# A routed feed-forward block with attention on one core: the first tile's copy, the late slots and two residual sums in another order

## The reference

```
x = x + 0.5 * ffn(layernorm(x))
x = x + attention(layernorm(x))        # 16 heads of 16, 4 key/value groups, causal
x = x + 0.5 * ffn(layernorm(x))

ffn(h):  route = sigmoid(h @ router_w)               # 8 experts
         e     = argmax(route), p = max(route)
         out   = p * (silu(h @ gate_w[e]) * (h @ up_w[e])) @ down_w[e]
```

## Time and profile before

| | us |
|---|---|
| median of three runs | 398.64 |
| lowest and highest run | 398.38, 400.58 |
| span of the profiled execution, first to last instruction | 397.6 |
| PE busy | 361.3 (91%) |
| DVE busy | 242.6 (61%) |
| POOL busy | 169.8 (43%) |
| ACT busy | 142.5 (36%) |

### The profile page before, as it was taken

How to read it: one execution, slowest core, us unless ns; L and a number is a source line. 1 busy time by engine, 2 the same in 40 slices (tenths; PEclk the granted TensorE clock), 3 DMA queues, 4 the chain that set the end, 5 groups by cost and what they waited for, 6 DMA issues and landing times.

```text
span 397.6 us, 8485 instructions
## 1 busy us (share of the span) xinstructions
PE 361.3 (91%) x3149; PEld 293.3 (74%) x3149; DVE 242.6 (61%) x773; ACT 142.5 (36%) x300; POOL 169.8 (43%) x291
## 2 busy tenths in 40 slices
PE   8679999999999778898999999899899999999980
PEld 4439999999967346576676666676599999999670
DVE  4887864222332766887989779789847874332220
ACT  2312111111120334675676757576434111111110
POOL 2040333565213243467767655565802424663111
PEclk9879999999999998999999999998989999999995
DMA  8959871249701644423616154100210111399100
GB/s 260 411 192 329 298 252 54 67 150 343 275 25 48 199 116 83 87 54 64 106 25 128 53 77 83 50 27 29 85 37 27 41 41 46 95 357 350 37 17 21
DMA packets 28099, 50.07 MB, mean 126 GB/s; under 512 B 4812, under 2 KB 21584, under 8 KB 27026
## 3 DMA queue, kind: packets, MB, share of 16 engines
q1 hardware_dynamic: 20082, 24.89, 22.7%
q0 software_dynamic: 4592, 21.76, 15.8%
q10 hardware_dynamic: 3376, 2.80, 2.4%
HBM read 34.95 MB, written 6.82 MB: 105 GB/s over the span
## 4 chain that ended last, share of the span: by engine, by line
PE 68%; DVE 20%; issue 3%; DMA 2%; SPq 2%; ACT 2%; ACTq 1%; POOL 1%; POOLq 0%; DVEq 0%
PE bank L1104 27%; PE bank L1130 14%; DVE mxa L1536 4%; PE bank L1347 4%; PE bank L577 3%; PE bank L1569 3%; PE bank L1519 3%; PE bank L1601 2%; PE bank L1094 2%; PE bank L1066 2%; PE bank L1630 2%; DVE area L1650 1%; SPq L1464 1%; DMA area<-x 1%; PE bank L1126 1%
## 5 line engine op out<-in xcount | busy, mean ns | idle before, releaser
L1104 PEld LDWEIGHTS bank<-area,W 128*128 128x128 f32 x1024 | 120.3, 194 | 4.0 <-ACT area L1207 2.5
L1104 PE MATMUL bank<-area,W 128*128 128x128 f32 x1024 | 121.2, 277 | 2.0 <-ACT area L1207 2.0
L1284 DVE TENSOR_TENSOR area<-area,bank 128x512 f32<-128x512 f32 x34 | 23.3, 687 | 68.8 <-issue 46.1
L1130 PE MATMUL bank<-W,area 128*128 128x256 f32 x256 | 60.9, 381 | 0.2 <-DVE area L1269 0.2
L1579 ACT ACTIVATE area<-bank 128x512 f32<-128x512 f32 x96 | 52.6, 597 | 19.0 <-PE bank L1569 18.8
L1588 POOL TENSOR_SCALAR_AFFINE_SELECT area<-area 128x512 f32<-128x512 f32 x64 | 40.6, 641 | 39.0 <-ACT area L1579 38.9
L1536 DVE TENSOR_REDUCE mxa<-bank 128x2 f32<-128x512 f32 (+2 forms) x96 | 51.8, 545 | 8.1 <-PE bank L1523 8.0
L1218 ACT ACTIVATE area<-bank 128x512 f32<-128x512 f32 x34 | 20.3, 597 | 97.9 <-PE bank L1104 91.4
L1130 PEld LDWEIGHTS bank<-W,area 128*128 128x128 f32 x256 | 46.1, 190 | 6.2 <-issue 1.2
L952 POOL DMA_INDIRECT out<-area,sidx x17 | 17.0, 1002 | 59.0 <-DVE area L1269 56.8
L952 POOL DMA_INDIRECT x2d<-area,sidx x17 | 16.9, 996 | 59.1 <-DVE area L1269 55.3
(11 more groups left out here) (209 smaller groups left out, 540.0 us busy)
## 6 DMA issues: line engine op xcount, KB each, us to landing
W<-wall SPq DMA_DIRECT2D x24, 512.0 KB, 6.5
area<-area SPq DMA_DIRECT2D x42, 128.0 KB, 3.8
area<-x SPq DMA_DIRECT2D x8, 256.0 KB, 5.7
area<-x2d SPq DMA_DIRECT2D x8, 256.0 KB, 4.5
rows<-area ACTq DMA_DIRECT2D x8, 256.0 KB, 2.8
area<-JV SPq DMA_DIRECT2D x40, 32.0 KB, 3.5
area<-area SPq DMA_DIRECT2D x12, 64.0 KB, 2.7
area<-x,gidx POOLq DMA_INDIRECT x18, 2.8
```

The costliest lines, as they stand in the source:

```text
L1104: last = pe.matmul(ps[:, i * P:(i + 1) * P], W[:, w:w + P], xT[:, j % 2, c, :], start=(c == 0), stop=(c == C - 1))
L1130: last = pe.matmul(y, hT[:, n % 2, i, :], W[:, bass.ds(off + at, H)] if mixed(n) else W[:, off + at:off + at + H], start=(i == 0), stop=(i ...
L1284: v.tensor_tensor(out, sil[:, n % 2, :], bank[2 + n % 2][:], ALU.mult).then_inc(f_h[l], 1)
```

## The change

It touches the first pass (l = 0) alone, though two tables are now indexed by pass.

- ScalarE: the exponential of the second phase, `route_exp(0, 1)`, stands behind `copy_tile(0)` and no longer ahead of it.
- VectorE: `finish(0)` stands ahead of `rest_positions` (tile 1) and `finish(1)` ahead of `rest_onehots` (tile 2). Of the value quarters, one stays ahead of `finish(2)` and two stand behind it. `slots` moves from tile 4 to tile 5 and `rest_experts` from 5 to 6; `normalise` runs two tiles ahead for one tile longer.
- TensorE: `rest_slots_pe` moves from tile 4 to tile 5.
- GpSimd: the first gather waits for `gidx` alone and not for `sidx` too. The wait for the second phase's slots and the gather of tile 8 stand one tile later.

```
-FIRST_B = (5, 6)
+FIRST_B = (6, 6)
+SLOT_STEP = (5, 6)
...
         def ffn_pool(l, seen):
             p = nc.gpsimd
-            p.wait_ge(s_ia[l], 2)
+            p.wait_ge(s_ia[l], 1)
...
                 gather(l, j)
+            p.wait_ge(s_ia[l], 2)
...
-                if j == SIDE[l] + 4:
+                if j == SLOT_STEP[l]:
                     rest_slots_pe(l, bank[4])
...
                 if j == 0:
                     copy_tile(0)
-                    if l == 1:
+                    if l == 0:
+                        route_exp(0, 1)
+                    else:
                         ln_evacuate(2, B - 1, bank[4])
...
-            ahead = SIDE[l] + 4
+            ahead = SLOT_STEP[l]
...
                 if j == SIDE[l]:
                     rest_places(l, seen, bank[7])
+                first = l == 0 and 1 <= j <= 2
+                if first:
+                    finish(j - 1)
                 if j == SIDE[l] + 1:
                     rest_positions(l, seen)
                 if j == SIDE[l] + 2:
                     rest_onehots(l)
                     rest_values(l, (0,))
                 if j == SIDE[l] + 3:
-                    rest_values(l, (1, 2, 3))
-                if j == SIDE[l] + 4:
+                    rest_values(l, (1,) if l == 0 else (1, 2, 3))
+                if j == SLOT_STEP[l]:
                     slots(l, 1, seen, bank[4])
-                if j == SIDE[l] + 5:
+                if j == SLOT_STEP[l] + 1:
                     rest_experts(l, seen)
-                if j >= 1:
+                if j >= 1 and not first:
                     finish(j - 1)
+                if l == 0 and j == SIDE[l] + 3:
+                    rest_values(l, (2, 3))
...
             logits_turn(2)
-            route_exp(0, 1)
             ffn_act(0)
```

## The result

In 17 runs each the change takes 398.19 us (median; 396.31 to 399.87) and the kernel before 399.59 (396.93 to 403.15). The ratio is 0.9966, with a 95% interval of 0.9950 to 0.9983: a gain of about 1.4 us, between 0.7 and 2.0, where 2.19 was forecast. The time lies above the forecast range (395.8 to 397.8). Two things are in that gap of 1.7 us: the kernel before is 0.95 us slower in 17 runs than in the three that the forecast started from, and the gain is smaller than forecast. Either alone would have left the time inside the range: 399.59 - 2.19 is 397.4, and 0.9966 of 398.64 is 397.3.

The account below looks back on a forecast made before the run. The prediction took TensorE to bound the kernel (68% of the path that ends last, VectorE 20%). Gains of 1.78 and 0.41 us, with late slots costing zero, made 2.19 off 398.64: 396.45, forecast 396.5, range 395.8 to 397.8.

Parts of the forecast that it names:

- Term 1, the copy: First pass, tile 0: with ScalarE's copy ahead of the exponential, gate and up start at 26.97, not 28.75; gain 1.78 us.
- The copy can start at about 26.57: ScalarE, tile 0: the transposed tile is ready at 26.55, so the copy could start then instead of at 28.35.
- Term 2, the sums: VectorE, first pass: finish(0) ahead of the positions removes TensorE's stall at the down projection of tile 1; gain 0.41 us.
- Term 3, the late slots: First pass: slots one tile later cost TensorE zero; the gather of tile 8, issued at 63.9, lands in time.
- starved tiles: Rival, chance 0.04: late slots delay the gather of tile 8, TensorE waits up to 5.5 us, time 402.0.
- a gain lost at the pass's end: Rival, chance 0.04: a transfer of scattered rows bounds the attention prologue, so nothing is left of the gain: 398.6.
- VectorE holding GpSimd up: Rival, chance 0.02: VectorE's operations delay GpSimd's scatter and gather ahead of tile 8; a large hold would bring back 398.6.
- The sum: Whole kernel: 1.78 + 0.41 = 2.19 us off the median of 398.64, giving 396.45.
- part of the gain: Case, chance 0.30: gain of 0.5 to 2.0 us, with VectorE's product or sum, or a late tile 8 gather, on the path.
- allowance of 0.3 us per meeting: GpSimd: extra time allowed when a gather runs beside VectorE's one-hots, after one took 1.21 us there.

Follow-up runs that it names:

- rest_only: The change with the exponential put back ahead of the copy of tile 0, against the kernel before: ratio 0.9962 (0.9940 to 0.9984), stretch 99.73 us.
- sums_back: The change with finish(0) and finish(1) put back behind the positions and one-hots, against the kernel before: ratio 0.9990 (0.9959 to 1.0020), stretch 98.97 us.
- keep12: The change with twelve more warm matmuls in TensorE's idle time from 12 to 15 us, against the kernel before: ratio 0.9969 (0.9940 to 0.9998).
- swap_only: The kernel before with only the copy of tile 0 moved ahead of the exponential, against the kernel before: ratio 0.9973 (0.9941 to 1.0004).

## Why the forecast went wrong

**Term 1, the copy.** The mechanism was right: the copy moved, the exponential kept its place behind VectorE's logits, the silu became bound by the table load (or tied with it) at no cost, the stall of 1.78 us went. The step that failed is "The copy can start at about 26.57". I took the transpose's start, 26.11, as set by `normalise(0)` (26.05). It was a tie: the warm matmuls ended at 26.13. I had read that and used it only for the two behind the transpose. A tie in one trace says nothing of which side moves between executions. Here TensorE's side moves: with a late clock, as in the first and third trace of the change, tile 0 starts 0.7 to 0.8 us late. Of the fourteen traces six show the hold with six or eight warm matmuls or with four; of the three of the unaltered change, two do. Their losses (0.76, 0 and 0.65 beyond the usual 0.06) average 0.47 us.

**Term 2, the sums.** 0.41 forecast; 0.41 in the trace of rest_only, 0.4 between sums_back and the change. VectorE's wait for the down projection ahead of `finish(0)` was 0.49 us, not under 0.1, in the first trace, which has a hold, and 0.15 in the second, which has none. It cost nothing.

**Term 3, the late slots.** Nothing, as forecast. GpSimd issued the gather of tile 8 at 63.11, 2.60 us behind the start of `finish(4)` (60.51), forecast 2.64, and it landed in 2.7 us; the transpose followed at 69.35 without a wait. `MIX` started at 110.02 without a wait. (The 54.29 that the forecast gives the slot matmuls in the kernel before is 54.13 in the earlier trace rows; nothing hangs on the difference.) The first gather, which no longer waits for `sidx`, starts 0.30 us behind `gidx` in place of 0.37: under 0.1, as forecast. The rivals of starved tiles and of a gain lost at the pass's end fell. That of VectorE holding GpSimd up fell as a cost, though the meeting itself is larger than I allowed (below).

**The sum.** Without a hold the change saves 100.14 - 97.99 = 2.15 us of the stretch, against 2.19 forecast. Less the average loss of 0.47 it is 1.7 us, or a ratio of 0.9958. The three measurements gave 0.9966, 0.9956 and 0.9957. So about a fifth of the forecast gain was not there, and the first measurement lies on its low side within its own interval. That the hold is worth 0.47 us on average rests on three traces; the times are too coarse to show it. The case "part of the gain", to which I gave 0.30, came about, but by neither of the mechanisms that I had put under it: no product or sum of VectorE and no late gather was on the path.

**The starting point.** The larger part of the miss is the baseline. Three runs had a median of 398.64; 17 had 399.59, and 31 to 35 in the later comparisons 399.51 to 400.19. I gave a range for the change's time only 2.0 us wide, made of mechanisms alone, around a median of three runs that spread over 2.2 us. That spread should have been in the range: it was in the table.

**Where the scatter sits.** From the first matmul behind the last tile to the transpose that opens the second pass it took 160.44 us before, 160.78, 160.36 and 160.72 in the three traces of the change, and 159.66 to 163.16 over all traces. The three longest (162.13 to 163.16) have the deepest dips of the granted clock in attention's prologue. keep12 (163.16):

```profile
130.00:140.00 10.00, 8.13 (x30) 5.08 (x31) 6.53 (x20) 3.85 (x8) 2.33 (x12) 0.83 0.64 198
145.00:150.00 5.00, 3.04 (x23) 2.19 (x24) 4.22 (x9) 2.21 (x6) 1.85 (x3) 0.96 0.49 93
150.00:155.00 5.00, 5.00 (x30) 3.87 (x29) 2.35 (x7) 0.99 (x3) 1.70 (x2) 0.70 0.61 119
```

The second trace of the change (160.36), the same places:

```profile
145.00:150.00 5.00, 3.26 (x26) 2.48 (x25) 3.73 (x8) 1.40 (x3) 2.60 (x3) 1.00 0.48 92
150.00:155.00 5.00, 4.09 (x35) 2.79 (x35) 4.00 (x11) 2.81 (x7) 2.18 (x4) 1.00 0.58 107
```

The dips don't explain all of it: swap_only took 159.68 us with a clock of 0.79 and 0.87 from 145 to 150 and 150 to 155 us, the first trace of the change 160.78 with 0.79 and 0.86. That the dips cause the longer stretch was not tested, only seen together; what decides in which execution the clock dips stays open.

**Best version.** The change with four or two warm matmuls has in its traces what the forecast promised, or nearly (stretches of 97.98, 98.21 and 98.00, the last two with a late clock). By the times none of these kernels can be told from the change, the first measurement of four apart.

## What to carry to other kernels

When a stall is removed, list everything that was ready within a tenth of a microsecond of the new start, filler work included, and ask which side varies between executions. Filler matmuls, put there to keep the clock up, are free only while something slower stands behind them; after each gain ahead of them their number has to be looked at again. Compare kernels by a stretch inside the trace that starts and ends at named instructions: here it repeated to 0.05 us, where the 95% intervals from 8 to 17 whole runs reached 0.7 to 1.4 us to either side.

## What the hardware showed unexpectedly

- **The clock's return wanders.** In the three traces of the change, one and the same program, TensorE was back at 2.4 GHz at 25.1, 23.1 and 24.9 us; over the thirteen traces in which it had fallen, anywhere from 22.2 to 25.4. The Trainium skill (TensorE: Matmul & The Clock Gate, "What's actually happening") says that the warm-up is run-variable, puts its penalty under 1% of a typical kernel and advises against fitting a specific count of cold matmuls. The traces agree that it varies, and 0.8 us of 397 is within that 1%; yet it was 0.8 us out of a gain of 2.2.
- **GpSimd beside VectorE's one-hots.** In the change the scatter and the gather that meet them took 1.64 and 1.86 us, where others take 1.0. The second and third traces show the same durations to 0.01 us:

```profile
43.51 1.64 POOL L953 DMA_INDIRECT x2d<-area,sidx  x1 [3.10 <-DVE area L1273]
45.46 1.86 POOL L941 DMA_INDIRECT area<-x,gidx  x1 [0.31 <-issue]
```

  That gather landed 7.8 us behind its issue, and `normalise(6)` waited 1.19 us for it; the kernel before has a wait of 1.20 at `normalise(5)`. `normalise(6)` ended at 53.65 and TensorE reached the transpose of that tile at 56.62, with 3 us in hand, so it did not matter. Against an allowance of 0.3 us per meeting the two took 0.6 and 0.9 more than usual.
- **No drain behind the table load.** In the second trace of the change the silu started at 28.46, 0.02 us behind the load's end (27.16 + 1.28), with its gate long there, so the switch of tables took 1.30 us. The Trainium skill (ScalarE: Activation LUTs, "What ACT_TABLE_LOAD costs") has 1283 ns of load, which agrees, and about 1380 ns of drain, 2.66 us in all, which does not.
